# Two gated attention layers: weighted sums once per head group, and a row stage that transposes fp32 rows

## The chip, the cores and the metric

One NeuronCore of one Trainium2 chip. The metric is device time of one execution in microseconds; lower is better. The kernel before took 1207.3 us (median of 3 runs, 1205.55 to 1210.32).

## What is computed

The input `x` has 32 batches of 256 rows of 256 channels, all fp32. Four blocks follow each other, each added to the running rows through a gate `tanh(g)` after a layer norm:

```python
x = x + tanh(g_xattn[0]) * attention(layernorm(x), ctx_2048, w_qkv, w_proj, b_proj)
x = x + tanh(g_ffn[0]) * ternary_linear(layernorm(x), weight, bias)
x = x + tanh(g_xattn[1]) * depool(layernorm(x), ctx_2048, patch_lens, W_in, b_in, g_res, g_init)
x = x + tanh(g_ffn[1]) * int8_linear(layernorm(x), rhs)
```

The attention has 16 heads of 16 channels; each of the 256 queries of a batch attends to 256 keys of the batch and 120 keys of the context (376 in all). The ternary linear layer rounds its rows by one scale for the whole tensor (so it can't begin before all batches have gone through the attention), clips them to -128..127 and multiplies them by weights of -1, 0, 1. The int8 layer rounds every row by its own scale. Integers of this size are exact in bf16.

## The kernel before, in words

There are two stages, each a software pipeline over the batches, with its order written out by hand on every engine: the attention stage (`*_attention`, iterated by `iterations`, with a hardware loop over b = 2 to 25 and the rest unrolled), then the row stage (`*_rows`, iterated by `row_iterations`, hardware loop over n = 12 to 31). Engines meet by semaphores only, and each works strictly in program order.

**Attention stage.** One iteration b is cut into HS = 24 units u. In unit u TensorE does, in this order: `scores_t(u)` (L596), two bf16 matmuls that give transposed scores of two heads for one of NKT = 3 tiles of keys, in one of SR = 3 PSUM banks `st_ps`; one or two `scores` (L606), which give plain scores for a row maximum (banks `ms_ps`, two); one piece of the jobs in the table `JOBS` (projections L644, L647, L652; transposes L636, L657, L662, L668, L673), and in odd units one `attend`. ScalarE takes the exponential of the transposed scores (`exp`, L883, 512 columns a time) into one of PR = 8 buffers `probs`. `attend(B, pB, w)` (L621) is a weighted sum: for a group of 4 heads (HG) and one tile of keys it does 4 fp32 matmuls with stationary operands of 32 columns, one in each quarter of the array's columns, adding over the 3 tiles of keys in `pv_ps`. An fp32 matmul shows as two records. So a head group takes three `attend` calls (w = 3g, 3g+1, 3g+2) in units 6g+3, 6g+5 and 6g+7 (the last group's last one falls in unit 1 of the next iteration). ScalarE copies `pv_ps` out (`copy_o`, L899) at units 8, 14, 20 and 2.

The row maxima are negated, split in three bf16 parts by GpSimd (`split_neg`, L472 to L478), transposed on TensorE (jobs neg0 at unit 20, neg1 at unit 8), copied by ScalarE (L891) and moved by a DMA from ScalarE's queue (L893) into rows of `q6`, so that `scores_t` has the maximum subtracted in the matmul.

Queries and keys are split in three bf16 parts by GpSimd too (L535 to L541, two halves m of the heads). SyncE stacks the parts into `q6` and `k6` with 12 DMAs for each half (`stack`, L396 and L398); TensorE waits for the first half at unit 6 of the next iteration (`scores`, wait on `d_stack`). GpSimd reaches L535 after the work that waits for VectorE's L842 (unit 17) and after `split_neg` of the maxima up to unit 17.

VectorE takes the row maxima (L789), normalises a head group (L796, L798) at units 5, 10, 16 and 22, adds the projection (L831, unit 12) and takes statistics (L818, L822, L836, L842, L844, L846).

**Row stage.** Iteration n works on batch n - offset for each step: ROUND0 = 1, MM0 = 2, UPD0 = 3, NORM1 = 4, MM1 = 5, UPD1 = 6, NORM3 = 7, QUANT = 8, MM2 = 9, SCALED = 10, FINAL = 11. Two of the steps round rows. For the ternary layer: ScalarE scales (L1269, `yq`, fp32), VectorE adds the constant ROUND = 1.5 * 2^23 and clips (L1195), ScalarE subtracts it into a bf16 copy `qq` (L1224), TensorE transposes that (L1087, bank `tq_ps`), and ScalarE copies it out (L1241, `qqT`) for the product (L1110). For the int8 layer the steps are L1262 (`y3`), the row maximum L1170, its scale L1177 and reciprocal L1184, L1203 (times the reciprocal, clip; two instructions), L1208 (plus ROUND, clip), then ScalarE's bf16 copy `q3` (L1230), transposes (L1092, `t3_ps`), L1247 and the product (L1115). GpSimd adds a bias (L1031, two instructions), derives the norms' factors (L1044 to L1051) and adds the last product (L1026, two instructions). All transposes of the stage stand in the helper line L1068, all plain products in L1074; the trace's name of `yq`, `y3` and others is `probs`, that of the bf16 copies `parts`, since they share their memory.

Of the kernel before, what the change touches and what calls it, by code (L numbers as in the profile page):

```python
# [14 lines left out]
def flamingo_two_layers(  # L15
# [22 lines left out]
    T = S // P  # L38
# [16 lines left out]
    PR = 8  # L55
# [23 lines left out]
    with ExitStack() as ctx:  # L79
# [110 lines left out]
        qq = [bparts[:, i * T * C:(i + 1) * T * C].rearrange("p (t c) -> p t c", t=T) for i in range(2)]  # L190
        q3 = [bparts[:, i * T * C:(i + 1) * T * C].rearrange("p (t c) -> p t c", t=T) for i in range(2, 4)]
# [67 lines left out]
        r_s = sem("r_s")  # L259
# [10 lines left out]
        r_s3 = sem("r_s3")  # L270
# [274 lines left out]
        def tensor_attention(pe):  # L545
# [38 lines left out]
            def body(i, par):  # L584
# [100 lines left out]
                for u in range(HS):  # L685
# [7 lines left out]
                    if u == 1 and live(b - 1):  # L693
                        attend(b - 1, opp, NG * NKT - 1)
                    elif u % 2 and u > 1 and live(b):
                        attend(b, par, (u - 3) // 2)
# [294 lines left out]
        tq_ps = ms_ps[0][:, :].bitcast(BF16)  # L991
        t3_ps = ms_ps[1][:, :].bitcast(BF16)
# [62 lines left out]
        def tensor_rows(pe):  # L1055
# [6 lines left out]
            def body(i, par):  # L1062
# [20 lines left out]
                if live(n - MM0):  # L1083
                    B, q = n - MM0, half(i, par, MM0)[1]
                    pe.wait_ge(r_s, B + 1)
                    wait(pe, r_cq, B)
                    transposes(tq_ps, qq[q], identb, r_tq)  # L1087
                if live(n - MM2):
                    B, q = n - MM2, half(i, par, MM2)[1]
                    pe.wait_ge(r_s3, B + 1)  # L1090
                    wait(pe, r_c3, B)
                    transposes(t3_ps, q3[q], identb, r_t3)  # L1092
# [24 lines left out]
            row_iterations(pe, body)  # L1117

        def vector_rows(dve):
# [23 lines left out]
            def body(i, par):  # L1143
# [22 lines left out]
                if has_q:  # L1166
                    Bq, qq_ = n - QUANT, half(i, par, QUANT)[1]
                    cq, y = Bq * 5, y3[qq_]
# [31 lines left out]
                if has_q:  # L1200
                    dve.wait_ge(r_q3, cq + 3)
                    for t in range(T):
                        ins = dve.tensor_scalar(y[:, t, :], y[:, t, :], am3[:, 1, t:t + 1], 127.0, ALU.mult, ALU.min)  # L1203
                    ins.then_inc(r_q3, 1)
                if has_q:

                    dve.wait_ge(r_q3, cq + 4)
                    dve.tensor_scalar(y, y, ROUND, ROUND - 127.0, ALU.add, ALU.max).then_inc(r_q3, 1)  # L1208
# [3 lines left out]
        def scalar_rows(act):  # L1212
            act.wait_ge(s_glob, 13)

            def body(i, par):
                n = i * 2 + par

                if live(n - MM0):

                    B, q = n - MM0, half(i, par, MM0)[1]  # L1220
                    act.wait_ge(r_q, B + 1)
                    if live(B - 2):
                        act.wait_ge(r_tq, B - 1)
                    act.activation(qq[q], yq[q], ACT.Relu, bias=cst[:, 0:1]).then_inc(r_s, 1)  # L1224
                if live(n - MM2):
                    B, q = n - MM2, half(i, par, MM2)[1]
                    act.wait_ge(r_q3, (B + 1) * 5)
                    if live(B - 2):
# [92 lines left out]
```

## Time and profile before

| | |
|---|---|
| runs | 1210.32, 1205.55, 1207.3 us; median 1207.3 |
| profiled execution | 1205.75 us; span in the profile 1204.0 us |
| TensorE / its weight loads | busy 1098.1 us (91%) / 667.5 us |
| VectorE, ScalarE, GpSimd | busy 930.2 (77%), 869.0 (72%), 698.9 us (58%) |
| granted TensorE clock | 0.972 of full speed over the span, full in the middle of both stages |
| attention stage | about 60 to 975 us |
| row stage | about 982 to 1204 us |

The profiled execution took 1.55 us less than the median of the runs. A row of the timeline has start, duration (both us), engine, line, operation and operands; "x2" merges two instructions that follow each other, and the bracket gives the idle time before and what ended it. TensorE's instructions overlap, so steps are read from start to start; the chain of waits gives such steps directly.

### The profile page before, as it was taken

What the parts mean: (1) busy time and instruction counts of PE and PEld (TensorE: products, weight loads), DVE (VectorE), ACT (ScalarE), POOL (GpSimd) and SP (SyncE); (2) the same over time, 40 slices, a digit from 0 to 9 for tenths busy, and PEclk for the clock granted to TensorE, in tenths of its full rate; (3) what the DMA queues carried; (4) which work ended last, traced back from release to release, by engine and by line L of the source; (5) the groups of instructions that cost most, each with busy time, mean ns of one, the idle gap of its engine ahead of it and who ended that gap; (6) DMA issues with size and microseconds to landing.
All of it is one profiled execution on the core that took longest, in us unless ns stands there. A gap on an engine that the chain in (4) does not pass through costs nothing.

```text
span 1204.0 us, 33614 instructions
## 1 busy us (share of the span) xinstructions
PE 1098.1 (91%) x8458; PEld 667.5 (55%) x8458; DVE 930.2 (77%) x2360; ACT 869.0 (72%) x1794; POOL 698.9 (58%) x1259
## 2 busy tenths in 40 slices
PE   3599999999999999999999999999999948878784
PEld 3355555555555555555555555555555426666663
DVE  3877777777777777777777777777777647999997
ACT  2167777777777777777777777777776658999984
POOL 5355555666555555555555666665554136777766
PEclk9599999999999999999999999999999978999997
DMA  4233334343433333333333333333333101222222
GB/s 131 73 93 96 97 99 103 101 101 103 105 102 102 101 102 98 108 101 95 95 95 95 98 102 102 100 103 99 98 91 87 38 21 42 77 84 80 79 86 80
DMA packets 158681, 110.19 MB, mean 92 GB/s; under 512 B 17154, under 2 KB 154788, under 8 KB 158628
## 3 DMA queue, kind: packets, MB, share of 16 engines
q1 hardware_dynamic: 156900, 108.78, 33.3%
q10 hardware_dynamic: 1728, 0.79, 0.2%
q8 instruction: 23, 0.38, 0.1%
q14 instruction: 30, 0.25, 0.1%
HBM read 30.30 MB, written 16.29 MB: 39 GB/s over the span
## 4 chain that ended last, share of the span: by engine, by line
PE 64%; DVE 15%; issue 9%; POOL 3%; DMA 2%; SPq 2%; ACT 2%; DVEq 1%; POOLq 0%; ACTq 0%
PE pv_ps L621 14%; PE ms_ps L606 13%; PE st_ps L596 12%; PE misc L644 9%; PE misc L652 5%; PE misc L647 4%; DVE neg L789 2%; PE aux L668 2%; DVE am L1170 2%; DMA q<-parts 2%; DVE xs L1159 2%; DVE probs L1203 1%; PE aux L673 1%; SPq L398 1%; PE aux L662 1%
## 5 line engine op out<-in xcount | busy, mean ns | idle before, releaser
L789 DVE TENSOR_REDUCE neg<-ms_ps 128x1 f32<-128x376 f32 x1024 | 531.9, 544 | 206.7 <-PE ms_ps L606 200.7
L883 ACT ACTIVATE probs<-st_ps 128x512 f32<-128x512 f32 x768 | 451.3, 599 | 173.7 <-PE st_ps L596 98.3
L606 PE MATMUL ms_ps<-k,q 96*128 96x376 bf16 x1024 | 336.0, 329 | 13.5 <-DVE neg L789 5.4
L596 PE MATMUL st_ps<-q,k 99*128 99x256 bf16 x1536 | 295.5, 274 | 0.1
L621 PE MATMUL pv_ps<-probs,v 128*32 128x256 f32 (+1 forms) x3072 | 245.4, 391 | 0.6 <-ACT oT L899 0.4
L596 PEld LDWEIGHTS st_ps<-q,k 99*128 99x128 bf16 x1536 | 134.5, 98 | 91.8 <-ACT probs L883 28.3
L606 PEld LDWEIGHTS ms_ps<-k,q 96*128 96x128 bf16 x1024 | 98.7, 96 | 144.7 <-DVE neg L789 79.0
L644 PE MATMUL misc<-xnT,wqkvT 128*128 128x256 f32 x512 | 156.8, 391 | 1.5 <-ACT xnT L904 1.5
L511 POOL TENSOR_TENSOR xs<-xs,bias_p 128x256 f32 (+1 forms) x64 | 45.2, 726 | 142.8 <-ACT xn L941 142.8
L621 PEld LDWEIGHTS pv_ps<-probs,v 128*32 128x32 f32 (+1 forms) x3072 | 60.5, 108 | 117.7 <-issue 93.1
L541 POOL TENSOR_TENSOR parts<-qk,parts 128x632 bf16<-128x632 f32 x64 | 88.7, 1386 | 13.2 <-POOL parts L539 13.2
L644 PEld LDWEIGHTS misc<-xnT,wqkvT 128*128 128x128 f32 x512 | 92.2, 197 | 6.6 <-ACT xnT L904 2.3
L537 POOL TENSOR_TENSOR qk<-qk,parts 128x632 f32<-128x632 f32 x64 | 88.6, 1384 | 11.7 <-POOL parts L535 11.7
L652 PE MATMUL misc<-wprojT,attnT 128*128 128x256 f32 x256 | 75.8, 378 | 0.8 <-ACT attnT L921 0.8
L647 PE MATMUL misc<-wqkvT,xnT 128*128 128x256 f32 x256 | 76.4, 379 | 0.0
L1100 PE MATMUL st_ps<-winT,probs 128*128 128x256 f32 x256 | 70.3, 397 | 6.0 <-ACT probs L1236 5.4
L515 POOL TENSOR_SCALAR plug<-plug,iota_n 120x256 f32<-120x256 f32 x32 | 36.9, 1154 | 48.1 <-DMA plug<-plugs 48.1
L1068 PE MATMUL ms_ps<-identb,parts 128*128 128x128 bf16 x256 | 26.8, 231 | 40.3 <-ACT parts L1230 25.2
L1100 PEld LDWEIGHTS st_ps<-winT,probs 128*128 128x128 f32 x256 | 46.8, 193 | 17.0 <-issue 7.9
L535 POOL TENSOR_SCALAR parts<-qk 128x632 bf16<-128x632 f32 x64 | 45.9, 718 | 13.9 <-issue 13.5
L539 POOL TENSOR_SCALAR parts<-qk 128x632 bf16<-128x632 f32 x64 | 46.1, 720 | 12.5 <-POOL qk L537 12.5
L899 ACT COPY oT<-pv_ps 128x256 f32<-128x256 f32 x128 | 47.8, 373 | 6.9 <-PE pv_ps L621 6.6
(187 smaller groups left out, 1775.3 us busy)
## 6 DMA issues: line engine op xcount, KB each, us to landing
k<-parts SPq DMA_DIRECT2D x384, 94.0 KB, 2.8
q<-parts SPq DMA_DIRECT2D x384, 64.0 KB, 2.5
xs<-in_x SPq DMA_DIRECT2D x32, 256.0 KB, 2.8
out_dram<-xn SPq DMA_DIRECT2D x32, 256.0 KB, 2.2
cx<-in_ctx SPq DMA_DIRECT2D x32, 240.0 KB, 3.4
recurrence_input<-u_in SPq DMA_DIRECT2D x32, 120.0 KB, 2.3
plug<-plugs SPq DMA_DIRECT2D x32, 120.0 KB, 3.4
powers<-gath SPq DMA_DIRECT2D x32, 120.0 KB, 3.2
```

Of the source, the lines that this page charges most:

```text
L537: pool.tensor_tensor(f, f, parts[:, m, 0, :], ALU.subtract).then_inc(s_split, 1)
L541: pool.tensor_tensor(parts[:, m, 2, :], f, parts[:, m, 1, :], ALU.subtract).then_inc(s_split, 1)
L596: mm = pe.matmul(st_ps[u % SR][:, j * S:(j + 1) * S], k6[0:KM, r, h, k * P:(k + 1) * P], q6[0:KM, r, h, :], start=True, stop=True)
L606: pe.matmul(ms_ps[t][:, 0:KEYS], q6[0:KR, r, h % HU, t * P:(t + 1) * P], k6[0:KR, r, h % HU, 0:KEYS], start=True, stop=True).then_inc(s_ms, 1)
L621: mm = pe.matmul(pv_ps[VW * j:VW * (j + 1), 0:S], v[0:rows, pB, k, HG * g + j, :], probs[0:rows, (2 * w + j // 2) % PR, j % 2 * S:(j % 2 + ...
L644: mm = pe.matmul(misc[:, x0 * S:(x0 + 1) * S], wqkvT[:, x1, at:at + P], xnT[:, par, x1, :], start=(x1 == 0), stop=(x1 == KT - 1), skip_gro ...
L647: mm = pe.matmul(misc[:, x0 * C:(x0 + 1) * C], xnT[:, opp, x1, x0 * P:(x0 + 1) * P], wqkvT[:, x1, 2 * C:3 * C], start=(x1 == 0), stop=(x1 ...
L652: mm = pe.matmul(misc[:, x0 * C:(x0 + 1) * C], attnT[:, x1, x0 * P:(x0 + 1) * P], wprojT[:, x1, :], start=(x1 == 0), stop=(x1 == KT - 1), ...
L789: dve.tensor_reduce(neg[:, m, t, h % HU:h % HU + 1], ms_ps[t][:, 0:KEYS], AX.X, ALU.max, negate=True).then_inc(s_red, 1)
L883: act.activation(probs[:, u % PR, :], st_ps[u % SR][:, :], ACT.Exp).then_inc(s_exp, 1)
L899: act.copy(oT[:, :], pv_ps[:, 0:S]).then_inc(s_oT, 1)
L1100: pe.matmul(m1_ps[q][:, t * C:(t + 1) * C], yxT[:, k, t * P:(t + 1) * P], winT[:, k, :], start=(k == 0), stop=False)
```

## The change

The weighted sums of a head group are issued together: the three `attend` calls stand in one unit (7, 13, 19, and 1 of the next iteration) and not in three, and `probs` has 12 buffers for 8. The sums themselves, their operands and their order are the same.

In the row stage the rounded fp32 rows (which still hold ROUND) are transposed directly with the fp32 identity, into fp32 banks, and ScalarE subtracts ROUND when it copies the transposed rows out to bf16. The bf16 copies `qq` and `q3` with their two ScalarE instructions (L1224, L1230) and semaphores go. VectorE's L1208 goes as well: L1203 becomes times-reciprocal, plus ROUND, with no clip. ScalarE's L1241 and L1247 read fp32 PSUM.

```diff
-    PR = 8
+    PR = 12
...
                     if u == 1 and live(b - 1):
-                        attend(b - 1, opp, NG * NKT - 1)
-                    elif u % 2 and u > 1 and live(b):
-                        attend(b, par, (u - 3) // 2)
+                        for k in range(NKT):
+                            attend(b - 1, opp, (NG - 1) * NKT + k)
+                    elif u % (2 * NKT) == 1 and u > 1 and live(b):
+                        for k in range(NKT):
+                            attend(b, par, (u // (2 * NKT) - 1) * NKT + k)
...
-        tq_ps = ms_ps[0][:, :].bitcast(BF16)
-        t3_ps = ms_ps[1][:, :].bitcast(BF16)
+        tq_ps, t3_ps = ms_ps
...
-                    pe.wait_ge(r_s, B + 1)
+                    pe.wait_ge(r_q, B + 1)
                     wait(pe, r_cq, B)
-                    transposes(tq_ps, qq[q], identb, r_tq)
+                    transposes(tq_ps, yq[q], ident, r_tq)
...
-                    pe.wait_ge(r_s3, B + 1)
+                    pe.wait_ge(r_q3, (B + 1) * 4)
                     wait(pe, r_c3, B)
-                    transposes(t3_ps, q3[q], identb, r_t3)
+                    transposes(t3_ps, y3[q], ident, r_t3)
...
                     for t in range(T):
-                        ins = dve.tensor_scalar(y[:, t, :], y[:, t, :], am3[:, 1, t:t + 1], 127.0, ALU.mult, ALU.min)
+                        ins = dve.tensor_scalar(y[:, t, :], y[:, t, :], am3[:, 1, t:t + 1], ROUND, ALU.mult, ALU.add)
                     ins.then_inc(r_q3, 1)
-                if has_q:
-
-                    dve.wait_ge(r_q3, cq + 4)
-                    dve.tensor_scalar(y, y, ROUND, ROUND - 127.0, ALU.add, ALU.max).then_inc(r_q3, 1)
...
-                    act.activation(qq[q], yq[q], ACT.Relu, bias=cst[:, 0:1]).then_inc(r_s, 1)
...
-                    act.activation(q3[q], y3[q], ACT.Identity, bias=cst[:, 1:2]).then_inc(r_s3, 1)
...
-                    act.activation(qqT, tq_ps[:, 0:KT * S].rearrange("p (k r) -> p k r", k=KT), ACT.Identity,
-                                   bias=cst[:, 2:3]).then_inc(r_cq, 1)
+                    act.activation(qqT, tq_ps[:, :].rearrange("p (k r) -> p k r", k=KT), ACT.Identity,
+                                   bias=cst[:, 1:2]).then_inc(r_cq, 1)
...
-                    act.copy(q3T, t3_ps[:, 0:KT * S].rearrange("p (k r) -> p k r", k=KT)).then_inc(r_c3, 1)
+                    act.activation(q3T, t3_ps[:, :].rearrange("p (k r) -> p k r", k=KT), ACT.Identity,
+                                   bias=cst[:, 1:2]).then_inc(r_c3, 1)
```

The reuse of `yq` and `y3` by ScalarE, which waited for the bf16 copies (`r_s`, `r_s3`), now waits for the transposes (`r_tq`, `r_t3`).

## Rows read from the trace of the kernel before

**Rows 1.** Busy time by stretch: start:end, length, then us busy of each engine.
```profile
400.00:600.00 200.00, 199.20 (x1618) 116.18 (x1616) 153.32 (x368) 148.94 (x317) 117.75 (x204) 1.00 0.37 100
...
1050.00:1100.00 50.00, 39.42 (x256) 30.85 (x255) 49.58 (x151) 46.61 (x88) 36.99 (x72) 1.00 0.26 80
```

**Rows 2.** Chain of waits, 500 to 530 us: start, step, engine, tile, line.
```profile
500.44 0.57 PE pv_ps L621 x8
...
502.89 0.27 PE ms_ps L606
...
503.37 0.16 PE ms_ps L606
503.53 0.43 PE misc L652 x2
```

**Rows 3.** Timeline of TensorE, one period of the attention stage.
```profile
501.17 0.33 PE L606 MATMUL ms_ps<-k,q 96*128 96x376 bf16 x1
...
502.25 0.64 PE L621 MATMUL pv_ps<-probs,v 120*32 120x256 f32 x8
...
509.36 0.64 PE L621 MATMUL pv_ps<-probs,v 120*32 120x256 f32 x8
...
514.12 0.32 PE L606 MATMUL ms_ps<-k,q 96*128 96x376 bf16 x1
...
529.58 0.32 PE L606 MATMUL ms_ps<-k,q 96*128 96x376 bf16 x1
```

**Rows 4.** Timelines of VectorE, GpSimd, SyncE's queue in the same period; landing of `q` DMAs.
```profile
515.00 0.24 DVE L842 BATCH_NORM_AGGREGATE mvt<-bn 128x2 f32<-128x6 f32 x2
...
518.83 0.72 POOL L535 TENSOR_SCALAR parts<-qk 128x632 bf16<-128x632 f32 x1 [0.50 <-issue]
...
526.78 0.60 SPq L396 DMA_DIRECT2D q<-parts  x1
...
DMA to landing us min/median/max: 2.3/2.5/3.3
```

**Rows 5.** Timeline of TensorE near 871 us, in the unrolled end.
```profile
871.45 0.33 PE L606 MATMUL ms_ps<-k,q 96*128 96x376 bf16 x1 [0.23 <-DMA q<-parts]
```

**Rows 6.** Timeline of ScalarE, units 8 to 11 of the same period.
```profile
504.22 0.36 ACT L891 COPY negT<-aux 24x256 bf16<-24x256 bf16 x1 [0.40 <-PE aux L662]
...
505.62 1.09 ACT L883 ACTIVATE probs<-st_ps 128x512 f32<-128x512 f32 x2 [1.04 <-issue]
...
507.99 0.60 ACT L883 ACTIVATE probs<-st_ps 128x512 f32<-128x512 f32 x1
```

**Rows 7.** Timelines of VectorE and GpSimd, two iterations of the row stage.
```profile
1080.72 0.39 DVE L1195 TENSOR_SCALAR probs<-probs 128x512 f32<-128x512 f32 x1
...
1086.61 0.85 DVE L1195 TENSOR_SCALAR probs<-probs 128x512 f32<-128x512 f32 x1
...
1088.15 0.46 DVE L1208 TENSOR_SCALAR probs<-probs 128x512 f32<-128x512 f32 x1
...
1091.88 0.63 DVE L1177 TENSOR_SCALAR ls<-am 128x2 f32<-128x2 f32 x1
...
1093.29 0.39 DVE L1195 TENSOR_SCALAR probs<-probs 128x512 f32<-128x512 f32 x1
...
1088.14 0.19 POOL L1044 TENSOR_SCALAR rn<-mv 128x2 f32<-128x2 f32 x1 [0.96 <-DVE mv L1199]
...
1091.76 1.42 POOL L1031 TENSOR_TENSOR xs<-xs,bias 128x256 f32 x2
```

**Rows 8.** Timeline of TensorE at the start and the end of the row stage.
```profile
988.47 0.61 PE L1068 MATMUL ms_ps<-identb,parts 128*128 128x128 bf16 x4 [0.56 <-ACT parts L1224]
...
993.82 1.12 PE L1068 MATMUL pv_ps<-ident,probs 128*128 128x128 f32 x4
...
1196.62 0.61 PE L1068 MATMUL ms_ps<-identb,parts 128*128 128x128 bf16 x4 [1.24 <-ACT parts L1230]
```

More of the change, by code:

```diff
@@ L189, in flamingo_two_layers @@
         bparts = parts[:, :, :, :].rearrange("p m a c -> p (m a c)")
-        qq = [bparts[:, i * T * C:(i + 1) * T * C].rearrange("p (t c) -> p t c", t=T) for i in range(2)]
-        q3 = [bparts[:, i * T * C:(i + 1) * T * C].rearrange("p (t c) -> p t c", t=T) for i in range(2, 4)]
         qqT = bparts[:, 4 * T * C:5 * T * C].rearrange("p (k r) -> p k r", k=KT)
@@ L258, in flamingo_two_layers @@
         r_q = sem("r_q")
-        r_s = sem("r_s")
         r_tq = sem("r_tq")
@@ L269, in flamingo_two_layers @@
         r_q3 = sem("r_q3")
-        r_s3 = sem("r_s3")
         r_t3 = sem("r_t3")
@@ L1167, in body @@
                     Bq, qq_ = n - QUANT, half(i, par, QUANT)[1]
-                    cq, y = Bq * 5, y3[qq_]
+                    cq, y = Bq * 4, y3[qq_]
                     dve.wait_ge(r_y3, (Bq + 1) * T)
@@ L1216, in body @@
                 n = i * 2 + par
[L1218 to L1223, printed above, removed]
-                    act.activation(qq[q], yq[q], ACT.Relu, bias=cst[:, 0:1]).then_inc(r_s, 1)
[L1225 to L1228, printed above, removed]
-                        act.wait_ge(r_t3, B - 1)
-                    act.activation(q3[q], y3[q], ACT.Identity, bias=cst[:, 1:2]).then_inc(r_s3, 1)
                 if live(n - MM1):
@@ L1259, in body @@
                     if live(B - 2):
-                        own_wait(act, r_s3, B - 1)
+                        own_wait(act, r_t3, B - 1)
                     for t in range(T):
@@ L1265, in body @@
                     if live(n - 2):
-                        act.wait_ge(r_s, n - 1)
+                        act.wait_ge(r_tq, n - 1)
                     for t in range(T):
```

## The prediction, made before the change had run

> **What bounds the kernel now.** I read the busy times by stretch first, then the chain of waits in the middle of each stage, then the timelines along that chain. In the attention stage TensorE is busy 199.2 of 200 us and no other engine above 77%; in the row stage VectorE is, 49.58 of 50 us [rows 1]. In the middle of the attention stage the chain runs through TensorE almost alone. Its period is that of the plain scores L606 of unit 6: 529.58 - 501.17 = 28.41 us for a batch [rows 3].
>
> But a second loop is nearly as long, and the reader should follow it, since it decides my forecast. From unit 6 (501.17) TensorE reaches the scores of unit 17 at 514.12 [rows 3], 12.95 us later. VectorE then does L842 at 515.00, GpSimd reaches the splitting L535 at 518.83, and SyncE issues the last stacking DMA of the first half at 526.78; it lands 2.5 us later, at 529.28 [rows 4]. That is what L606 of the next unit 6 waits for, and it ran at 529.58. With some 0.05 us for the semaphore the slack is 0.25 us in 28.41. Where a DMA issue is late, the wait shows [rows 5]. So TensorE can be sped up as much as one likes: the period falls only by 0.25 us unless the piece from unit 6 to unit 17 gets shorter too. The 14.3 us from L842 to the landing hold no work that the change touches.
>
> **Part 1, the sums together.** One call takes a step of 0.57 us on the chain, and the L606 behind it takes 0.27 for 0.16: 0.68 us. An fp32 product with the same two passes takes 0.43 [rows 2]. So 0.25 us of each call is the change between operations of 32 columns and whole ones. Twelve calls become four groups of three, 8 changes fewer, 2.0 us per batch of TensorE's time, if a call inside a group costs 0.43. No row shows such a call; its ends are 0.43 and 0.57, and I take 0.43, as all quarters of the array are in use in either case.
>
> Now the piece that matters. It held 5 calls (units 7, 9, 11, 13, 15), and now holds 6 in two groups. Unit 6 to the call in unit 7 is 1.08 us, unchanged. From there to the call of unit 13 it was 7.11 us with three calls [rows 3]: 7.11 - 3 x 0.68 + (3 x 0.43 + 0.25) = 6.61. But the group of unit 13 needs the exponential of unit 11. ScalarE's series to it starts with the negated maxima (L891 at 504.22), which TensorE transposes in unit 8, after the call of unit 7; then comes the DMA issue, the exponential at 505.62 and, without a gap, that of unit 11, over at 508.59 [rows 6]. The group in unit 7 ends 2 x 0.43 = 0.86 us later than the single call did, and the series moves with it: 509.45, with 0.05 us to reach TensorE 7.25 us to the next group, not 6.61. So TensorE waits 0.64 us here. From unit 13 to unit 17 it was 4.76 us with two calls, now 4.76 - 1.36 + 1.54 = 4.94. Together 13.27 us against 12.95: 0.32 longer, less the slack of 0.25, and the period grows by 0.07 us. Some 30 batches stack a successor: **+2.1 us**. Bounds: without ScalarE's lateness the piece is 0.64 shorter, -0.57 per batch, -17 us. With 0.57 us for inner calls, 4 of them in the piece, it is +0.63 per batch, +19 us.
>
> Twelve buffers for `probs` only uphold this: the exponential of unit 18 needs the sums of unit 13. DMA issues are untouched. VectorE gets two scores late during a group of 1.4 us, covered by its 23% of idle time; should it fall behind before L842, that adds to the loop. At the end of the stage all three last sums come after the last exponential: 2 x 0.43, **+0.9 us**.
>
> The Trainium skill says (TensorEngine Tiling, Key Properties) that changing the tiling mode drains TensorE; the 0.25 us above agrees. Read alone it promises the whole 2.0 us per batch.
>
> **Part 2, the row stage.** Two iterations take 1093.29 - 1080.72 = 12.57 us, 6.29 each [rows 7]. VectorE loses L1208: 0.46 busy, about 0.4 us of its path, as the next instruction starts before its end. ScalarE loses two instructions and had idle time; TensorE's fp32 transposes cost it perhaps 0.4 us per iteration and it is busy 39.4 of 50 [rows 1], so both cost nothing: the cover is VectorE's remaining 5.9 us. If that cover went, TensorE would need 0.79 + 0.08 of 1.
>
> Against it stands GpSimd. L1195 takes 0.39 us in one iteration and 0.85 in the next, and L1177, an operation on 2 columns, 0.63: it ends at 1092.51, just past the middle of GpSimd's pair at 1091.76 [rows 7]. So each iteration holds one wait of 0.46 us for GpSimd's running instruction of 0.7 us. GpSimd's block in turn begins (1088.14) when L1203 is over, at the start of L1208. Without L1208 VectorE's next iteration begins there, and GpSimd's block comes 0.4 us later against VectorE's. Then L1177 and L1195 can both meet it: two waits of 0.35 on average are 0.7 for 0.46, +0.24; both in full are +0.94, none is -0.46. I take a little more than the average, +0.3: -0.1 us an iteration, 20 in the loop, **-2 us** (-17 to +11).
>
> The Trainium skill (SBUF — State Buffer, SBUF: two separate sides) has it that VectorE and GpSimd share a pair of ports under a lock that is held for a whole instruction. The trace agrees: 0.85 us for 0.39, up to the end of GpSimd's instruction.
>
> Ends of the stage: at its start the transposes wait for L1224 [rows 8], in a loop over two iterations that loses it; some 0.5 us in 3 iterations, -1.5. Three iterations before L1026 begins lose L1208 freely, -1.2. Six draining ones lose perhaps 0.3 each, -1.8. On the last batch L1208, L1230 (0.72) and a hand-over go, -1.25, and the fp32 transposes at the lower clock cost 1.12 for 0.61 [rows 8], +0.5: -0.75. Together **-5.2 us**.
>
> **Sum.** +2.1 + 0.9 - 2 - 5.2 = -4.2, against the profiled execution's 1205.75: 1201.6. The median stands 1.55 above it, so 1203 us.
>
> **Rivals.**
> 1. TensorE's saving lands in part. If ScalarE's series isn't late (its DMA issue or its copies overlap better), the piece shrinks: -0.57 per batch, 1203 - 2 - 17 = 1184 us. For it: TensorE is the busiest engine by far. Against: the series is gapless from 505.62 on. 0.20.
> 2. TensorE's whole saving lands, 8 changes of 0.25 us in each of some 31 batches: 62 us, 1203 - 2 - 62 = 1139. That needs the stacking to start earlier, and nothing in the change does that. 0.05. (It is what the Trainium skill's TensorEngine Tiling, Key Properties, would lead to by itself.)
> 3. Slower: the loop unit 6, ScalarE's exponential of unit 11, unit 17, VectorE, GpSimd, SyncE gets longer by more than I counted, through dearer inner calls or VectorE reaching L842 late. At 0.35 us per batch more, 30 x 0.35 = 10.5: 1213.5; at both bounds, 1222. It decides from 0.2 us per batch over my sum on. 0.17.
> 4. The waits for GpSimd eat more than L1208 gives: +0.3 us an iteration instead of -0.1 makes 20 x 0.4 = 8, so 1211. 0.08.
>
> **Chances.** The forecast itself (1198 to 1211) has 0.50. A measurement of this kernel can tell about 0.5%, 6 us, from no change; so it is faster below 1201.3 and slower above 1213.3. Faster: 0.20 + 0.05 + a fifth of the forecast's own, 0.35. Slower: most of rival 3 and a part of rival 4 and of the forecast's upper end, 0.21. Same: 0.44. The range goes from under rival 1 to past 0.35 us per batch in rival 3: 1180 to 1218 us. The forecast's own range is 1198 to 1211.
>
> **What would show it.** Right: the chain of waits in the attention stage, TensorE alone before, goes every batch through L842, L535, SyncE's queue and a DMA on `q`; TensorE is idle before L606 of unit 6; its busy share falls to some 93% while the period stays within 0.2 us of 28.4; and it waits some 0.6 us for an exponential before the group of unit 13. The row stage: two waits per iteration on L1177 and L1195, period near 6.2. Wrong: a period under 28.0 in the attention stage, or a stack of DMAs that is issued earlier; a group of sums that takes clearly more than 1.5 us; a row period near 5.9, which would mean that the waits for GpSimd didn't grow.

## The result, and the profile after

The changed kernel takes 1215.3 us (median of 6 runs, 1211.3 to 1219.3), the kernel before 1207.3 us (median of 5 runs, 1205.6 to 1210.3; a sixth took 5038.7 us, for a cause that isn't known, and is left out): ratio 1.0064, 95% interval 1.0043 to 1.0084. It is slower by some 8 us, near the upper end of the range of 1180 to 1218 and on the other side of the forecast of 1203. The profiled execution took 1211.31 us with a span of 1209.5.

Two figures split the difference: the starts of VectorE's projection add, once a batch, whose last one all but ends the attention stage, and the span. These are the groups of that line, the kernel before first; "DVEq" is its sequencer in the loop, with 24 batches between the two starts shown.

```profile
L831 DVE SCALAR_TENSOR_TENSOR xs<-misc,tg,xs x32: 741/742/751, 109.7 to 975.2; 128x512 f32 x24, 128x512 f32<-128x512 f32 x8
L831 DVEq FUSED_REGOPS  x24: 57/57/57, 138.5 to 793.2; - x24
```

```profile
L829 DVE SCALAR_TENSOR_TENSOR xs<-misc,tg,xs x32: 741/743/752, 110.0 to 995.7; 128x512 f32 x24, 128x512 f32<-128x512 f32 x8
L829 DVEq FUSED_REGOPS  x24: 57/57/57, 139.5 to 811.7; - x24
```

From its first add to its last the attention stage grew from 865.5 to 885.7 us, by 20.2 us; its period in the loop went from (793.2 - 138.5) / 23 = 28.47 to (811.7 - 139.5) / 23 = 29.23 us. What follows the last add shrank from 1204.0 - 975.2 = 228.8 to 1209.5 - 995.7 = 213.8 us, by 15.0. So two large effects of opposite sign hide behind 0.6%. Busy times by stretch, which answer to [rows 1]:

```profile
400.00:600.00 200.00, 188.60 (x1570) 117.98 (x1570) 151.89 (x360) 143.69 (x310) 114.24 (x196) 1.00 0.36 97
1050.00:1100.00 50.00, 44.42 (x276) 36.28 (x274) 50.00 (x155) 40.87 (x77) 39.41 (x76) 1.00 0.27 82
```

TensorE has fallen from 199.2 to 188.6 us busy of 200 and yet each batch takes longer: it waits. The chain of waits over one batch, which answers to [rows 2], says for what (start, step, engine, tile, line):

```profile
500.42 0.23 PE aux L658 x2
500.67 0.37 ACT negT L889
...
501.14 2.73 DMA q<-negT
...
504.00 0.39 PE st_ps L592 x2
...
508.81 0.46 DVE neg L787
...
511.41 0.30 DVE attn L796
...
511.85 0.63 PE aux L669 x4
...
516.10 2.67 DMA q<-negT
```

Before, this chain was TensorE almost alone (it went through VectorE once, near 510 us). Now it leaves TensorE twice a batch for a round trip: TensorE transposes the negated maxima (L658), ScalarE copies them (L889) and issues a DMA of 12 KB that takes 2.7 us, and the scores product of unit 0 or 12 can't start earlier. In between it goes to VectorE, for a maximum (L787) and for the normalised rows (L796). The waits of TensorE from 400 to 800 us, in total, their number and the longest:

```profile
PE st_ps L592 <- DMA q<-negT: 11.2, 26, 0.7
PE ms_ps L602 <- DVE neg L787: 5.3, 27, 0.2
PE aux L669 <- DVE attn L796: 4.7, 13, 0.4
```

None of the three was in the same view of the kernel before. These totals are idle time as the profile models it; the steps from start to start tell the whole price. I add up the steps of TensorE's timeline by what the instruction does, over six whole batches from after 400 us, and divide by six (us for a batch; "sums" are the weighted sums, "products" the projections, "plain scores" the L606 or L602, "scores" the transposed ones, L596 or L592, "rest" the transposes). A wait counts to the instruction that stands before it:

| kernel | sums | products | plain scores | scores | rest | period |
|---|---|---|---|---|---|---|
| before | 6.87 | 7.92 | 5.64 | 5.63 | 2.37 | 28.42 |
| changed | 5.75 | 7.68 | 6.87 | 6.29 | 2.58 | 29.18 |

The sums take 1.12 us less. The products' steps give 0.24 less with one wait of 0.38 us among them (before the scores of unit 12), so 0.62 without it: TensorE saves some 1.7 us of work a batch. But the steps behind plain scores and scores, which hold other waits, are 1.23 and 0.66 us longer, and the rest 0.21. These are TensorE's rows of one period, which answer to [rows 3]:

```profile
500.35 0.28 PE L658 MATMUL aux<-identb,negp 128*24 128x128 bf16 x2
...
504.00 0.39 PE L592 MATMUL st_ps<-q,k 99*128 99x256 bf16 x2 [0.61 <-DMA q<-negT]
...
510.36 0.32 PE L602 MATMUL ms_ps<-k,q 96*128 96x376 bf16 x1
...
511.17 0.32 PE L602 MATMUL ms_ps<-k,q 96*128 96x376 bf16 x1
511.85 0.63 PE L669 MATMUL aux<-ident,attn 128*128 128x128 f32 x4 [0.36 <-DVE attn L796]
...
512.79 1.50 PE L617 MATMUL pv_ps<-probs,v 128*32 128x256 f32 x24
...
515.31 0.28 PE L658 MATMUL aux<-identb,negp 128*24 128x128 bf16 x2
...
518.89 0.39 PE L592 MATMUL st_ps<-q,k 99*128 99x256 bf16 x2 [0.22 <-DMA q<-negT]
...
519.96 1.50 PE L617 MATMUL pv_ps<-probs,v 128*32 128x256 f32 x24
...
524.98 0.32 PE L602 MATMUL ms_ps<-k,q 96*128 96x376 bf16 x1
```

**What had covered the round trips** shows in the same stretch of the kernel before, from the transposes of the maxima in unit 8 to the scores product of unit 12, and from those in unit 20 to the scores product of the next unit 0. The first row is the plain scores of unit 5, of which the account of the prediction makes use:

```profile
499.68 0.32 PE L606 MATMUL ms_ps<-k,q 96*128 96x376 bf16 x1
...
503.90 0.28 PE L662 MATMUL aux<-identb,negp 128*24 128x128 bf16 x2
...
508.29 0.39 PE L596 MATMUL st_ps<-q,k 99*128 99x256 bf16 x2
...
518.38 0.28 PE L662 MATMUL aux<-identb,negp 128*24 128x128 bf16 x2
...
522.33 0.39 PE L596 MATMUL st_ps<-q,k 99*128 99x256 bf16 x2
```

The first took 4.39 us, with two single sums (units 9 and 11) in it, and the changed kernel, which waits for its end, shows a round trip of 3.58 (515.31 to 518.89). The second took 3.95 us, with the sums of units 21 and 23 in it, for a round trip of 3.65 (500.35 to 504.00): 0.8 and 0.3 us to spare. Two single sums are 2 x 0.68 us. Without them TensorE is there too early, and waits, longer where there was less to spare.

In the row stage VectorE is the engine that matters, busy 50.00 of 50 us. Its rows, which answer to [rows 7]:

```profile
1086.97 0.15 DVE L1176 TENSOR_SCALAR ls<-am 128x2 f32<-128x2 f32 x1
...
1087.90 0.78 DVE L1194 TENSOR_SCALAR probs<-probs 128x512 f32<-128x512 f32 x1
...
1088.76 0.94 DVE L1202 TENSOR_SCALAR probs<-probs,am 128x256 f32<-128x256 f32 x2
...
1092.96 0.72 DVE L1176 TENSOR_SCALAR ls<-am 128x2 f32<-128x2 f32 x1
...
1094.47 0.39 DVE L1194 TENSOR_SCALAR probs<-probs 128x512 f32<-128x512 f32 x1
...
1094.93 0.58 DVE L1202 TENSOR_SCALAR probs<-probs,am 128x256 f32<-128x256 f32 x2
1095.43 0.86 DVE L1152 SCALAR_TENSOR_TENSOR probs<-st_ps,ls,w1s 128x256 f32<-128x256 f32 x2
```

From L1202 to the next iteration's first instruction is 0.50 us where no wait for GpSimd is in it (1094.93 to 1095.43). The waits stretch L1194 by 0.39 and L1202 by 0.36 in one iteration and L1176 by 0.57 in the next: 1.32 for two, 0.66 for one, where it was 0.46.

### The profile page after: what moved, and what is told of

Same layout as the page of the kernel before. It is cut to its first block, busy times and chain, and to the rows that moved or that the text cites. A ratio compares the mean times of both kernels' runs of the same rounds, so it can differ in the third digit from the quotient of the medians.

```text
span 1209.5 us, 33412 instructions
## 1 busy us (share of the span) xinstructions
PE 1081.5 (89%) x8458; PEld 704.0 (58%) x8458; DVE 921.8 (76%) x2328; ACT 824.3 (68%) x1730; POOL 700.1 (58%) x1259
## 4 chain that ended last, share of the span: by engine, by line
PE 46%; DVE 20%; DMA 13%; issue 11%; POOL 3%; ACT 3%; SPq 3%; DVEq 2%; POOLq 0%; ACTq 0%
PE pv_ps L617 14%; DMA q<-negT 10%; PE ms_ps L602 9%; PE st_ps L592 7%; DVE neg L787 4%; PE misc L640 4%; PE misc L643 3%; PE misc L648 2%; DVE bn L834 2%; DVE am L1169 2%; PE aux L669 2%; DVE xs L1158 2%; ACT negT L889 1%; DMA q<-parts 1%; SPq L394 1%
## 5 line engine op out<-in xcount | busy, mean ns | idle before, releaser
L787 DVE TENSOR_REDUCE neg<-ms_ps 128x1 f32<-128x376 f32 x1024 | 530.0, 544 | 222.2 <-PE ms_ps L602 216.6
L881 ACT ACTIVATE probs<-st_ps 128x512 f32<-128x512 f32 x768 | 443.9, 602 | 134.1 <-PE st_ps L592 124.2
L602 PE MATMUL ms_ps<-k,q 96*128 96x376 bf16 x1024 | 335.5, 328 | 27.5 <-DVE neg L787 17.2
L592 PE MATMUL st_ps<-q,k 99*128 99x256 bf16 x1536 | 294.9, 273 | 23.2 <-DMA q<-negT 21.3
L592 PEld LDWEIGHTS st_ps<-q,k 99*128 99x128 bf16 x1536 | 136.6, 98 | 112.5 <-ACT probs L881 30.9
L617 PE MATMUL pv_ps<-probs,v 128*32 128x256 f32 (+1 forms) x3072 | 194.1, 385 | 0.1
L602 PEld LDWEIGHTS ms_ps<-k,q 96*128 96x128 bf16 x1024 | 98.7, 96 | 134.0 <-DVE neg L787 67.7
L617 PEld LDWEIGHTS pv_ps<-probs,v 128*32 128x32 f32 (+1 forms) x3072 | 87.2, 110 | 80.5 <-issue 20.8
L643 PE MATMUL misc<-wqkvT,xnT 128*128 128x256 f32 x256 | 79.5, 391 | 0.0
L1097 PE MATMUL st_ps<-winT,probs 128*128 128x256 f32 x256 | 67.1, 384 | 0.7 <-ACT probs L1217 0.7
L1065 PE MATMUL ms_ps<-ident,probs 128*128 128x128 f32 x256 | 44.0, 300 | 22.1 <-DVE probs L1194 14.2
L531 POOL TENSOR_SCALAR parts<-qk 128x632 bf16<-128x632 f32 x64 | 46.1, 720 | 13.8 <-issue 13.5
L468 POOL TENSOR_SCALAR negp<-neg 128x16 bf16<-128x16 f32 x64 | 13.1, 205 | 68.5 <-DVE neg L787 68.4
```

Source lines behind the costliest of these rows:

```text
L592: mm = pe.matmul(st_ps[u % SR][:, j * S:(j + 1) * S], k6[0:KM, r, h, k * P:(k + 1) * P], q6[0:KM, r, h, :], start=True, stop=True)
L602: pe.matmul(ms_ps[t][:, 0:KEYS], q6[0:KR, r, h % HU, t * P:(t + 1) * P], k6[0:KR, r, h % HU, 0:KEYS], start=True, stop=True).then_inc(s_ms, 1)
L617: mm = pe.matmul(pv_ps[VW * j:VW * (j + 1), 0:S], v[0:rows, pB, k, HG * g + j, :], probs[0:rows, (2 * w + j // 2) % PR, j % 2 * S:(j % 2 + ...
L643: mm = pe.matmul(misc[:, x0 * C:(x0 + 1) * C], xnT[:, opp, x1, x0 * P:(x0 + 1) * P], wqkvT[:, x1, 2 * C:3 * C], start=(x1 == 0), stop=(x1 ...
L787: dve.tensor_reduce(neg[:, m, t, h % HU:h % HU + 1], ms_ps[t][:, 0:KEYS], AX.X, ALU.max, negate=True).then_inc(s_red, 1)
L881: act.activation(probs[:, u % PR, :], st_ps[u % SR][:, :], ACT.Exp).then_inc(s_exp, 1)
```

## The experiments

Ratios are to the kernel before on the same chip. "Period" is the attention loop's, from the same two rows of the projection add as above.

| kernel | us | ratio (95%) | period |
|---|---|---|---|
| sums_only | 1227.1 | 1.0150 (1.0126 to 1.0173) | 29.23 |
| rows_only | 1197.0 | 0.9908 (0.9887 to 0.9929) | 28.49 |
| rows_pr12 | 1196.7 | 0.9916 (0.9902 to 0.9929) | 28.46 |
| merge_only | 1199.4 | 0.9941 (0.9927 to 0.9954) | 28.49 |
| fp32T_only | 1205.3 | 0.9985 (0.9974 to 0.9996) | 28.46 |
| late_groups | 1269.6 | 1.0509 (1.0485 to 1.0533) | 31.13 |
| stats_last | 1207.2 | 0.9991 (0.9977 to 1.0005) | 28.99 |
| late_fixed | 1211.2 | 1.0039 (1.0025 to 1.0053) | 29.11 |
| aT_later | 1215.9 | 1.0070 (1.0051 to 1.0089) | 29.23 |
| neg_first | 1193.2 | 0.9880 (0.9860 to 0.9900) | 28.51 |
| neg_first_aT | 1188.8 | 0.9829 (0.9809 to 0.9849) | 28.47 |
| single_neg_first | 1209.4 | 1.0009 (0.9996 to 1.0022) | 29.03 |
| pairs | 1189.8 | 0.9873 (0.9851 to 0.9896) | 28.43 |
| pairs_stats | 1191.7 | 0.9879 (0.9860 to 0.9899) | 28.49 |
| rows_stats | 1188.7 | 0.9855 (0.9836 to 0.9874) | 28.41 |

### The two halves by themselves

sums_only has the first part of the diff alone (the grouped `attend` calls, `PR = 12`), rows_only the second alone.

> The kernel before with the first half of the change alone: the sums of a head group in one unit, 12 buffers; the row stage as before. From the two traces the attention stage lost about 0.76 us for each batch in the loop and the row stage gained 15 us. If both halves act alone, this is 1207 + 20 = 1227 us (ratio 1.017). If the halves interact (a memory layout, the hand-over between the stages), it lies clearly elsewhere, below 1220 or above 1235.

> The kernel before with the second half alone: the row stage of the change, sums and 8 buffers as before. If the halves act alone: 1207 - 15 = 1192 us (ratio 0.988), and a row period near 5.9 us with waits of 0.65 us an iteration for GpSimd. If most of the gain came from elsewhere in the changed kernel, about 1203, as my prediction's own sum for this half (-7.2) said.

The halves multiply to 1.0150 x 0.9908 = 1.0057, within the interval of the whole. So there is no sign that they act on each other: the grouping costs 19 us, the row stage gives 11.

rows_pr12 is rows_only with `PR = 12`:

> The row half alone with the old single sums, as in rows_only (1197.0 us), but with 12 probability buffers in place of 8. Theory (the buffers only make the grouping possible and neither gain nor cost by themselves): attention period 28.4 to 28.5 us, 1195 to 1199 us. Rival (part of the 20 us that the grouped sums cost is the buffers, by an exponential that runs earlier and takes ScalarE ahead of the negated copies, or by placement in memory): above 1201 us.

It equals rows_only. The buffers do nothing; the loss is the grouping.

### The row half, divided

merge_only, against the kernel before (the clamps are left out with it):

```diff
-  dve.tensor_scalar(y[:, t, :], y[:, t, :], am3[:, 1, t:t + 1], 127.0, ALU.mult, ALU.min)
+  dve.tensor_scalar(y[:, t, :], y[:, t, :], am3[:, 1, t:t + 1], ROUND, ALU.mult, ALU.add)
-  dve.tensor_scalar(y, y, ROUND, ROUND - 127.0, ALU.add, ALU.max).then_inc(r_q3, 1)
```

> The kernel before, with VectorE's clamping instruction L1208 gone and its addition folded into L1203; bf16 copies and their transposes stay, and so do the single sums. The edit leaves out the lower and upper clamps. Theory (the whole drop of the row period, 6.29 to 5.91 us, is this instruction): row period 5.9, some 27 iterations of 0.38 us, so 10 us less, and the ends of the stage keep the copies: about 1198 us. Rival (the copies on ScalarE hold part of the loop): row period 6.0 to 6.2, 1201 to 1205 us.

fp32T_only is the row half with these two lines left as they were.

> The kernel before, with the fp32 transposes of the rounded rows and without the bf16 copies, but with VectorE's two-step rounding kept. Theory: row period unchanged at 6.29 us, since VectorE has the same instructions; the ends of the stage gain 2 to 5 us: 1203 to 1206 us. Rival (the copies were part of the loop): period 6.0 to 6.2, under 1202 us.

The reduction L1170 (L1167, L1169) starts once an iteration. Its groups from about 1085 us on, of fp32T_only and the changed kernel:

```profile
L1167 DVE TENSOR_REDUCE am<-probs x7: 668/669/677, 1087.7 to 1125.4; 128x2 f32<-128x512 f32 x7
```
```profile
L1169 DVE TENSOR_REDUCE am<-probs x8: 667/670/674, 1085.7 to 1127.2; 128x2 f32<-128x512 f32 x8
```

Periods of 6.28 and 5.93 us, where it was 6.29; over the same stretch merge_only has 6.09 and rows_only 6.03. The fp32 transposes leave the loop alone and give 2.9 us at its ends (225.9 us after the last add, for 228.8). merge_only alone gives 6.9 by the same measure, and the two together 12.1 in rows_only and 15.0 in the changed kernel, more than their sum of 9.8. The loop of merge_only gave 0.2 us per iteration there, not the 0.38 I expected, and rows_only and the changed kernel have the same row stage and differ. rows_only's timeline of VectorE shows what differs:

```profile
1076.78 0.37 DVE L1174 TENSOR_SCALAR ls<-am 128x2 f32<-128x2 f32 x1
...
1077.94 0.85 DVE L1192 TENSOR_SCALAR probs<-probs 128x512 f32<-128x512 f32 x1
...
1082.72 0.73 DVE L1174 TENSOR_SCALAR ls<-am 128x2 f32<-128x2 f32 x1
...
1084.23 0.84 DVE L1192 TENSOR_SCALAR probs<-probs 128x512 f32<-128x512 f32 x1
```

Here the waits for GpSimd are 0.22 + 0.46 + 0.58 + 0.45 = 1.71 us for two iterations, 0.86 for one, against 0.66 in the changed kernel. The code is the same; the two engines meet in another phase. That isn't a property of the kernel: merge_only changes from one phase to the other within its execution.

```profile
1049.59 0.67 DVE L1170 TENSOR_REDUCE am<-probs 128x2 f32<-128x512 f32 x1
...
1055.41 0.67 DVE L1170 TENSOR_REDUCE am<-probs 128x2 f32<-128x512 f32 x1
...
1061.71 0.67 DVE L1170 TENSOR_REDUCE am<-probs 128x2 f32<-128x512 f32 x1
...
1067.64 0.67 DVE L1170 TENSOR_REDUCE am<-probs 128x2 f32<-128x512 f32 x1
```

The iteration before these took 5.99 us (from 1043.60), and then come 5.82, 6.30 and 5.93. Two iterations take 11.8 us in the one phase and 12.2 in the other, in merge_only and rows_only alike, and 11.8 in the changed kernel; the 0.4 between them is the 1.71 - 1.32 of the waits. The changed kernel's profiled execution stays in the faster phase, merge_only's and rows_only's are mostly in the slower one. So the bf16 copies hold no part of the loop, and the periods of 6.09 and 6.03 are mixtures. What starts a phase isn't shown.

### Does the place of the group matter?

late_groups, against the changed kernel:

```diff
-  if u == 1 and live(b - 1):
+  if u == 2 and live(b - 1):
-  elif u % (2 * NKT) == 1 and u > 1 and live(b):
+  elif u % (2 * NKT) == 2 and u > 2 and live(b):
```

ScalarE's copies of the sums follow, from units 2, 8, 14, 20 to 3, 9, 15, 21.

> The changed kernel with the group of sums one unit later (units 8, 14, 20 and 2, behind the transposes of the negated maxima in units 8 and 20), and ScalarE's copies of the sums one unit later too. Cover theory (the single calls used to fill TensorE's time while the negated maxima go through ScalarE's copy and a DMA of 2.7 us; grouped in unit 7 and 19 they stand ahead of that round trip and not inside it): the waits of 0.78 and 0.38 us before the scores of units 0 and 12 go, about -1.1 us per batch, 1215 - 33 = 1182, if no other loop holds it. Stack theory of the prediction (unit 6 to 17, VectorE, GpSimd, SyncE, DMA sets the period): that piece still holds two groups, so the period stays within 0.4 us of 29.2, 1203 to 1215 us.

It is 5% slower than before. TensorE's waits from 400 to 800 us:

```profile
PE st_ps L592 <- DMA q<-negT: 16.2, 13, 1.3
PE aux L658 <- POOL negp L474: 15.0, 13, 1.2
PE ms_ps L602 <- DVE neg L787: 14.2, 39, 0.6
```

The round trip to unit 0 is at once longer: its transposes now wait for GpSimd's split of the maxima, and ScalarE's copy of the sums stands ahead of its copy of the maxima. So this run tests neither theory: it adds waits of its own. stats_last is the changed kernel with GpSimd's statistics block (L515 to L518, a copy, an addition and a power for the next norm) moved from ahead of the splits of the maxima to behind the splitting for the stack:

```diff
-  pool.tensor_copy(mv1[:, bass.ds((b - 1) * T, T), :], mvt[:, :, :]).then_inc(s_std, 1)
...
   pool.tensor_tensor(parts[:, m, 2, :], f, parts[:, m, 1, :], ALU.subtract).then_inc(s_split, 1)
+  pool.tensor_copy(mv1[:, bass.ds((b - 1) * T, T), :], mvt[:, :, :]).then_inc(s_std, 1)
...
```

> The changed kernel with GpSimd's four statistics instructions (those that wait for VectorE's aggregates of unit 17, and the power) moved behind the splitting of queries and keys. They take 1.4 us of GpSimd ahead of the split, so the stacking DMAs are issued up to 1.4 us sooner. Stack theory: the period falls by what the stack loop was over the next bound, 0.2 to 0.8 us per batch, 1190 to 1209 us. Cover theory: TensorE isn't held by the stack, the period stays 29.2, 1213 to 1217 us, and the slack before the scores of unit 6 grows.

late_fixed joins the two and also puts ScalarE's copy of the maxima in unit 20:

> As late_groups (sums grouped in units 8, 14, 20, 2), with what held that kernel taken away: GpSimd's statistics behind the splitting, so that the negated maxima are split 1.4 us earlier, and ScalarE's copy of the transposed maxima of the first half in unit 20, ahead of its copy of the sums. Cover theory: the group now lies inside the round trip of the maxima, the waits on the negT DMA before the scores of units 0 and 12 vanish, period 28.0 to 28.6 us, 1180 to 1197 us. If the waits on VectorE (statistics, normalisation ahead of the transposes of unit 6) are what a group of sums costs, wherever it stands, the period stays at 28.9 or above, 1205 or more.

stats_last gives 8 us against the changed kernel, and its 1207.2 us lies in the range that I gave to the stack theory, not in that of the cover theory. But the changed kernel's list of waits above has no row for a DMA on `q` from `parts`, the stack's, and none for GpSimd's split of the maxima: TensorE waited for neither from 400 to 800 us. What changed in stats_last is one of the two waits for the negated maxima (6.5 us in 14, for 11.2 in 26). Before unit 12 the scores product comes 3.21 us after the transposes (511.31 to 514.52), without a wait, where the changed kernel needed 3.58. So the transfer took at most 2.4 us from its issue and not 2.8. The round trip isn't a fixed length. Moving GpSimd's block also moved the stack's DMAs: SyncE issues the last of them 0.5 us before this transfer in stats_last (511.58 and 512.11), and 0.9 us behind it in the changed kernel (516.99 and 516.10). That points to what else is in flight, but no run tests it. The period fell by a third of the loss, to 28.99.

late_fixed has no wait for the DMA left, but:

```profile
PE ms_ps L602 <- DVE neg L787: 19.4, 41, 0.7
...
```

In that order TensorE finds VectorE late instead, and the rival of that run was right: 1211.2 us, 29.11. The waits changed places, and I took this for the general rule; the next runs say where it holds.

### Which wait holds the period?

aT_later, against the changed kernel; the condition is that of ScalarE's copy of the transposed rows:

```diff
-  "aT": (1, 6, 1, -1),
+  "aT": (1, 7, 1, -1),
-  if u == 6 and live(b - 1):
+  if u == 7 and live(b - 1):
```

> The changed kernel, with the transposes of the normalised rows (aT) and ScalarE's copy of them one unit later (unit 7, ahead of the group of sums, in place of unit 6), so that VectorE's maximum, reciprocal and normalising product have one unit more before TensorE needs them. Theory (the grouped sums uncovered this wait of 0.52 us in each batch, which lies in the piece from unit 6 to unit 17 that the prediction took for unchanged): no wait of TensorE for VectorE's attn, piece 6 to 17 about 13.3 us, period 28.7 us in place of 29.23, and some 15 us less, 1200 us. Rival (the waits only change places: what TensorE saves here it loses before the maxima or the second DMA of negated maxima): period 29.1 to 29.2 us, 1212 to 1216 us.

The wait for the normalised rows is gone and the period is 29.23 us as before. Waits of TensorE, 400 to 800 us:

```profile
PE st_ps L592 <- DMA q<-negT: 9.3, 15, 0.8
PE st_ps L592 <- ACT probs L881: 8.0, 13, 0.7
...
```

The step before unit 12 took all of the gain. The profile puts its end down to an exponential, but the changed kernel starts the same product (518.89) before that exponential is over (518.61 + 0.61), so it can't be needed; the other condition is the DMA, 3.2 us after its issue here and 2.8 there. The stack's last DMA is issued 1.2 us behind it here (517.18 and 515.95), later than in both kernels above, which fits; but why it took longer isn't shown, and so this run doesn't say whether the wait for the normalised rows would count by itself. So I started the round trip itself earlier. neg_first, against stats_last, makes the two transposes the first job of their units, and puts ScalarE's copy ahead of the exponential of unit 20 where it stood behind it:

```diff
+  "neg1": (1, 8, 1, 0), "neg0": (1, 20, 1, 1),
   "xT": (0, 0, 1, 2),
...
-  if u == 21 and live(b + 1):
+  if u == 20 and live(b + 1):
       neg_rows(b + 1, opp, 0, live(b))
```

> The kernel stats_last (the changed kernel with GpSimd's statistics behind its splitting; 1207.2 us, period 28.99 us), with the transposes of the negated maxima as the first job of units 8 and 20, ahead of a projection step of 0.43 us, and with ScalarE's copy and DMA issue for unit 20 ahead of that unit's exponential. Theory (the round trip of the negated maxima, 3.6 us from the transposes to the next scores product, ends some 0.4 to 0.6 us after TensorE could go on, twice a batch, since no single sum stands in it any more): the waits before units 0 and 12 go, period 28.1 to 28.5 us, 1188 to 1196 us. Rival (the waits change places, to VectorE's maxima or elsewhere): period 28.8 to 29.0 us, 1203 to 1208 us.

> neg_first, and aT with ScalarE's copy of it in unit 7 as in aT_later. Theory (once the round trip of the negated maxima is out of the way, the wait of 0.5 us for the normalised rows counts): 0.2 to 0.5 us per batch less than neg_first, 5 to 12 us. Rival (it changes places again): within 2 us of neg_first, or slower, since ScalarE's copy then stands ahead of the negated maxima.

> The same earlier start of the negated maxima in rows_stats (single sums, the changed row stage, statistics behind the splitting; 1188.7 us, period 28.41 us). Theory (the single sums of units 9, 11, 21 and 23 cover the round trip, with some 0.8 us to spare before unit 12): no change, 1186 to 1191 us, period 28.4 us. Rival (the round trip costs the single sums something too): period under 28.2 us, under 1184 us.

neg_first takes 1193.2 us: 14 us less than stats_last. Its waits, 400 to 800 us:

```profile
PE ms_ps L603 <- DVE neg L788: 5.5, 28, 0.2
PE aux L670 <- DVE attn L797: 5.0, 14, 0.4
...
```

The DMA's row is gone, the other two stand as they were, and the period went from 28.99 to 28.51. So the round trip of the negated maxima held the grouped kernel above 28.5 us. Below that, waits do change places: the work that TensorE has left would fit in 28.42 - 1.74 = 26.7 us, so neg_first still waits 1.8 us a batch. neg_first_aT takes the row for L797 out of the list, and a row for an exponential grows from 1.6 to 3.4 us; its period is the same within 0.04 us. It takes another 4 us at the median (5 to 12 forecast), though its profiled execution is only 1 us shorter; that part isn't placed. What holds the grouped kernels at 28.5 us isn't shown.

The control missed. I expected no change for the single sums and got 20 us more. One wait is new (400 to 800 us):

```profile
PE pv_ps L618 <- ACT oT L896: 6.0, 14, 0.4
```

ScalarE's copy of the maxima now stands ahead of its copy of the sums in unit 20, and with single sums the next one (unit 21) needs the bank that this copy frees. With groups no sum follows until unit 1. So this run says that the edit has a price of its own with single sums; it doesn't say how much cover the single sums left. For that there are only the rows (4.39 us for 3.58, 3.95 for 3.65).

### Is there a better version?

pairs is rows_only with the first two sums of a head group in the unit of the second, the third alone; pairs_stats and rows_stats are pairs and rows_only with the statistics block behind the splitting.

```diff
-  attend(b, par, (u - 3) // 2)
+  w = (u - 3) // 2
+  if w % NKT:
+      if w % NKT == 1:
+          attend(b, par, w - 1)
+      attend(b, par, w)
```

> The row stage of the change, 8 buffers, and of each head group's three sums the first two together in the unit of the second; the third alone as before. Four mode changes fewer a batch, 1.0 us of TensorE. Stack theory: the piece from unit 6 to unit 17 hardly changes and the slack was 0.25 us, so at most 0.25 us a batch is won, against 1197 for the row half alone: 1189 to 1197. Cover theory: the smaller block leaves a call in the long gap before units 0 and 12, so nothing new waits, but VectorE's bursts lose one of the breaks they had; the same range, or up to 5 us slower than 1197 where they show.

> pairs, with GpSimd's statistics behind the splitting (the stack loop 1.4 us shorter). Stack theory: now TensorE's saving lands, up to 1.0 us a batch: 1197 - 30 = 1167 at best, 1170 to 1182 likely. Cover theory alone: VectorE's waits take most of it, 1185 to 1197.

> The row half of the change with GpSimd's statistics behind the splitting and the sums as before. TensorE alone bounds this attention stage at 28.4 us, so both theories say no gain: 1195 to 1198. A gain of 5 us or more would mean that the stack loop already held the kernel before, over its slack of 0.25 us.

Pairs save four changes between operations of 32 columns and whole ones, and the table of steps shows the same trade in small, this time even:

| kernel | sums | products | plain scores | scores | rest | period |
|---|---|---|---|---|---|---|
| rows_only | 6.85 | 7.92 | 5.63 | 5.64 | 2.38 | 28.41 |
| pairs | 6.29 | 7.51 | 5.61 | 6.44 | 2.53 | 28.38 |
| neg_first | 5.75 | 7.33 | 6.70 | 6.27 | 2.46 | 28.51 |

1.0 us saved, 0.9 waited, mostly for VectorE's maxima. The profiled execution of pairs is 7 us shorter than that of rows_only (4 by the ratios), and that lies outside the loop: 972.3 - 793.0 = 179.3 us from the loop's last add to the last of all, for 978.7 - 793.3 = 185.4. One batch there takes 31.7 us in rows_only and 28.3 in pairs; rows_pr12, which times like rows_only, has 182.4. rows_stats (1188.7 us) gains there too, against its forecast of no gain: the batches near the start and the end that took 29.1 to 31.7 us in rows_only, where TensorE waits for the stack's DMA (3.9 us in all from 800 us on), take 28.4. In the middle of the loop both take 28.41, so the stack held single batches at the ends and not the loop. pairs_stats, for which the stack theory had 1170 to 1182 us, takes 1191.7 with a period of 28.49: with the stacking shorter and 1.0 us less for TensorE to do, nothing came of it. That is the second run against the stack as the bound of the loop.

Three versions end near 1189 us: single sums with the statistics moved (rows_stats, ratio 0.9855), pairs (0.9873), and groups of three with three other edits (neg_first_aT, 0.9829). They ran on different chips, so the ratios are what compares; the intervals of the first and the last overlap. All are faster than both kernels. That grouping helps once its waits are gone isn't shown: the lowest ratio is a grouped one, by 3 us, and the loop's period is no shorter in it.

## Why the prediction was wrong

**The step that failed** is in part 1: "Unit 6 to the call in unit 7 is 1.08 us, unchanged", and with it the assumption behind all of that part, that taking sums out of a stretch can only make TensorE early, and that being early is free wherever the stacking loop leaves room. The two round trips of the negated maxima were priced only as ScalarE's lateness towards the group of unit 13; their wait before the scores products of units 12 and 0 had no term. By pieces, with the rows above:

- Unit 6 to the group of unit 7: 512.79 - 511.17 = 1.62 us, not 1.08. TensorE waits for L796. Before, the single sum of unit 5 stood between the plain scores at 499.68 and the transposes at 501.33, 1.65 us; now it is 510.36 to 511.85, 1.49 us, and without the wait it would be 0.97. VectorE's maximum, reciprocal and product need the 1.49.
- Unit 7 to unit 13: 519.96 - 512.79 = 7.17 us, forecast 7.25. The later start of the negated maxima is in it, as I had it, but the wait is another one: 0.38 us before the scores of unit 12, on the DMA, and not 0.64 before the group, on the exponential of unit 11. The forecast without any wait was 6.61, and 0.14 us of the rest is the step before the scores of unit 11, which waits for an exponential. That the sum comes so near is in part luck.
- Unit 13 to unit 17: 524.98 - 519.96 = 5.02, forecast 4.94. The group's own step is 1.43 us, as put (0.57 + 2 x 0.43).
- So the piece is 13.81 us, not 13.27: 0.54 over the forecast.
- Unit 17 to the next unit 6: I held it at 15.2 us, bounded by the stacking, with TensorE far ahead. It takes 29.21 - 13.81 = 15.40 us. TensorE alone, seven single calls becoming two groups, would have 15.46 - 7 x 0.68 + 2 x 1.54 = 13.8; it waits 1.6 us, half of it for the other round trip (0.78 at 504.00). The reserve that I thought would cover any wait was used up by it.

0.54 + 0.19 is the 0.73 us by which the period is over my 28.48. Over the 23 periods of the loop that makes 17 us, and 17.2 is what the stage is over the forecast (20.2, forecast +3.0). TensorE's saving was 1.7 us per batch (1.12 in the sums, 0.62 in the products), forecast 2.0. That the period would not fall was right. That a rival "slower" would come from the loop over unit 11, unit 17 and the stacking was half right: its price (1213.5 from 0.35 us per batch) is near, and the piece from unit 6 to unit 17 did get longer. But the stack isn't what TensorE waits for: the sign that I had named, TensorE idle before the plain scores of unit 6 for a DMA on `q` from `parts`, didn't come from 400 to 800 us; stats_last, with the stacking earlier, keeps two thirds of the loss in the loop, and neg_first takes nearly all of it away (28.51 us).

"VectorE gets two scores late ..., covered by its 23% of idle time" fell with it. The idle time is real (151.9 of 200 us busy) but lies elsewhere: while a group runs VectorE has nothing to do (idle for 1.15 us up to 507.14), and then it gets its maxima in a burst, behind two banks.

TensorEngine Tiling, Key Properties, of the Trainium skill names the drain at a change of mode; the trace agrees that there is such a cost, and the runs show that its saving was no saving in time here.

**Part 2** had the mechanism and a size off. It gave 15.0 us, forecast 7.2. The reduction L1170 (now L1169) starts 32 times and divides it:

```profile
L1170 DVE TENSOR_REDUCE am<-probs x32: 670/674/681, 1011.1 to 1193.0; 128x2 f32<-128x512 f32 x32
```
```profile
L1169 DVE TENSOR_REDUCE am<-probs x32: 666/671/677, 1029.2 to 1199.2; 128x2 f32<-128x512 f32 x32
```

From the last projection add to its first start it is 35.9 and 33.5 us, 2.4 less (forecast 1.5 for the stage's start), and behind its last start 11.0 and 10.3, 0.7 less (forecast 0.75). The 31 periods between took 181.9 and 170.0: 11.9 us, 0.38 each, where I had 0.1 in 20 of them and 3.0 for the ones before and behind (5.0 in all). L1208 took 0.55 us of VectorE's path, not 0.4: from L1203 to the next L1153 was 1.05 us on average, and is 0.50. The waits for GpSimd grew by 0.2 us, forecast 0.3 (and the plain average that I had worked out, 0.24, was nearer); in the slower phase they grow by 0.4. The row period near 5.9 that I named as a sign of error came, though not for the reason that I gave with it: the waits did grow.

## What to carry to other kernels

When an edit takes work out of an engine at the bound, list every round trip (copy, DMA, another engine's chain) that starts and ends on it, and read from the timeline how much of the removed work stood inside each. Work inside a round trip is cover, and can be removed only as far as the slack of that round trip goes (0.8 and 0.3 us here). To remove more, first start the round trip earlier. And where two halves of a change lie in different stages, run each alone: here +1.5% and -0.9% made 0.6%.

## What the runs showed of the hardware

- VectorE and GpSimd can meet in different phases with the same code, and change over within one execution: two iterations of the row stage take 11.8 or 12.2 us, with 1.32 or 1.71 us of VectorE's waits for GpSimd.
- A DMA of 12 KB issued by ScalarE took 2.7 us until its reader might start (501.14 and 516.10 above), about the same as the stack's of 64 KB (2.5 us) [rows 4]. In other versions the same DMA took at most 2.4 us (stats_last) and 3.2 us (aT_later) from its issue to its reader's start; the later the stack's last DMA was issued beside it, the longer it took, in these three.
- 12 fp32 products on 32 columns in a row (24 records) step 1.43 us: the 0.57 of four alone [rows 2] and twice 0.43. Each change between such products and whole ones that the grouping saved was worth 0.14 us in the sums and 0.08 in the products ahead of them (1.12 and 0.62 us for 8).
